# A decoder layer's router: exponential from a hyperbolic tangent, an earlier table load, and the first expert's two products in front of its low parts

## The reference, cut to what matters

```python
logits = x @ router_weight.T + router_bias              # 512 tokens x 16 experts
top_val, top_idx = jax.lax.top_k(logits, 4)
top_val = jax.nn.softmax(top_val, axis=-1)
router_scores = zeros_like(logits).at[arange(T)[:, None], top_idx].set(top_val)
gate_up = einsum('th,ehd->etd', x, gate_up_proj) + gate_up_proj_bias[:, None, :]
gate = minimum(gate_up[..., ::2], 7); up = clip(gate_up[..., 1::2], -7, 7)
glu = gate * sigmoid(gate * 1.702)
out = einsum('etd,edh->eth', (up + 1.0) * glu, down_proj) + down_proj_bias[:, None, :]
out = (out * router_scores.T[:, :, None]).sum(axis=0)
```

## Time and profile before

| what | value |
|---|---|
| median of 3 runs | 230.55 us (229.61 to 231.19) |
| the profiled execution's own time | 230.47 us |
| its span | 228.6 us |
| granted TensorE clock, mean of the span | 0.993 |
| PE busy | 216.3 us (95%) |
| DVE, ACT, POOL busy | 173.0, 127.8, 87.8 us |

### The profile page before, as it was taken

How to read it: one execution, slowest core, us unless ns; L and a number is a source line. 1 busy time by engine, 2 the same in 40 slices (tenths; PEclk the granted TensorE clock), 3 DMA queues, 4 the chain that set the end, 5 groups by cost and what they waited for, 6 DMA issues and landing times.

```text
span 228.6 us, 4527 instructions
## 1 busy us (share of the span) xinstructions
PE 216.3 (95%) x1466; PEld 180.2 (79%) x1466; DVE 173.0 (76%) x434; ACT 127.8 (56%) x247; POOL 87.8 (38%) x67
## 2 busy tenths in 40 slices
PE   7899989998799799989999999999999999999995
PEld 2577857876478599768878988988988988998994
DVE  3489876779357755688798898898889789779655
ACT  2128999874343412835847657566476485395440
POOL 6622269941001100044254455447428428428000
PEclk9999999999799999999999999999999999999999
DMA  5993042000000000004214304404412322310002
GB/s 145 323 409 125 1 140 94 3 4 0 0 0 3 0 0 3 1 0 139 67 73 139 133 4 138 138 7 131 138 40 97 138 57 80 138 46 0 0 3 92
DMA packets 7998, 17.43 MB, mean 76 GB/s; under 512 B 928, under 2 KB 3120, under 8 KB 7856
## 3 DMA queue, kind: packets, MB, share of 16 engines
q1 hardware_dynamic: 7232, 16.52, 21.5%
q10 hardware_dynamic: 752, 0.73, 1.3%
HBM read 16.72 MB, written 0.52 MB: 75 GB/s over the span
## 4 chain that ended last, share of the span: by engine, by line
PE 74%; DVE 10%; ACT 6%; DMA 4%; issue 3%; ACTq 1%; DVEq 0%
PE PS L1121 35%; PE PS L1137 19%; DMA mask<-mask_d 4%; PE PS L1008 3%; PE PS L993 3%; ACT pr L418 3%; DVE masked L692 2%; PE PS L964 2%; PE PS L950 2%; PE PS L981 2%; PE PS L1166 2%; PE PS L1088 1%; DVE HL L813 1%; PE PS L936 1%; PE PS L1020 1%
## 5 line engine op out<-in xcount | busy, mean ns | idle before, releaser
L301 POOL TENSOR_TENSOR WLg<-raw_g,WHg 128x1024 fp32r<-128x1024 f32 x16 | 41.1, 2570 | 61.1 <-ACT WHg L388 61.1
L1121 PE MATMUL PS<-XH,WHg 128*128 128x512 f32 x120 | 47.0, 392 | 0.4 <-ACT pt L503 0.4
L1121 PE MATMUL PS<-XL,WHg 128*128 128x512 f32 x120 | 46.9, 390 | 0.0
L1121 PE MATMUL PS<-XH,WLg 128*128 128x512 f32 x120 | 46.7, 389 | 0.0
L813 DVE TENSOR_TENSOR HL<-pt,HH 128x512 fp32r<-128x512 f32 x30 | 30.8, 1026 | 12.2 <-ACT HH L512 12.2
L512 ACT ACTIVATE HH<-pt 128x512 fp32r<-128x512 f32 x30 | 18.9, 631 | 36.7 <-DVE pt L808 35.7
L808 DVE SCALAR_TENSOR_TENSOR pt<-pt 128x512 f32<-128x512 f32 x30 | 36.2, 1205 | 4.2 <-DVE pt L804 1.6
L1137 PE MATMUL PS<-WHd,HH 128*128 128x256 f32 x120 | 34.2, 285 | 0.9 <-DVE HL L813 0.8
L1137 PE MATMUL PS<-WLd,HH 128*128 128x256 f32 x120 | 34.0, 283 | 0.0
L1137 PE MATMUL PS<-WHd,HL 128*128 128x256 f32 x120 | 33.9, 283 | 0.0
L308 POOL TENSOR_TENSOR WLd<-raw_w,WHd 128x512 fp32r<-128x512 f32 x15 | 22.1, 1473 | 16.7 <-ACT WHd L394 16.7
(11 more groups left out here) (149 smaller groups left out, 357.9 us busy)
## 6 DMA issues: line engine op xcount, KB each, us to landing
raw_g<-we_d SPq DMA_DIRECT2D x16, 512.0 KB, 3.9
raw_w<-we_d SPq DMA_DIRECT2D x16, 256.0 KB, 2.7
ctxT<-ctxT_d SPq DMA_DIRECT2D x1, 1024.0 KB, 11.6
ctx_sb<-ctx_d SPq DMA_DIRECT2D x1, 1024.0 KB, 13.7
wqkv<-wqkv_d SPq DMA_DIRECT2D x3, 256.0 KB, 6.5
out_d<-x SPq DMA_DIRECT2D x4, 128.0 KB, 1.8
rows<-rows_d ACTq DMA_DIRECT2D x1, 264.0 KB, 6.3
x<-x_d ACTq DMA_DIRECT2D x2, 128.0 KB, 3.1
```

What stands on the lines that cost most here:

```text
L301: g.tensor_tensor(WLg[slot][:, :, :, :].rearrange("p k g f -> p (k g f)"), raw_g[slot][:, :], WHg[slot][:, :, :, :].rearrange("p k g f -> ...
L1121: i = t.matmul(PS[:, 2 * m + part, :], w[slot][:, k, part, m * P:(m + 1) * P], xx[:, k, :], start=(n == 0), stop=(n == 3 * KD - 1))
```

## The change

Three things are changed.

1. `elog` becomes tanh(`dlog` / 8). DVE works the exponential out of it: with t = tanh(d / 8), (1 + t) / (1 - t) = exp(d / 4), whose fourth power is exp(d). That takes five more DVE instructions on 128 x 64 values: 1 - t (`root`), its reciprocal, (1 + t) times that, and two squarings.
2. The table set that holds the gate's function and the tangent is loaded by a `preload_act_table_set` in ACT's code, after `context_take(3)`.
3. In expert 0, DVE runs `product(0)`, `product(1)`, `low(0)`, then the copy of `scoreT`, then `low(1)`. Before it ran `product(0)`, the copy, `low(0)`, `product(1)`, `low(1)`. The other experts keep their order.

```diff
@@ scalar engine
             context_take(3)
+            a.preload_act_table_set("gelu_apprx_sigmoid_and_others")
             act.wait_ge(xs_done, NC)
             high_tokens(6, 10, slice(S, S + P), xh_done)
             high_tokens(4, 11, slice(S + P, T), xh_done)
             act.wait_ge(dlog_done, 1)
-            a.activation(elog[:, :, :], dlog[:, :, :], ACT.Exp).then_inc(elog_done, 1)
+            a.activation(elog[:, :, :], dlog[:, :, :], ACT.Tanh, scale=0.125).then_inc(elog_done, 1)
@@ vector engine, router
             link(i)
+            dve.wait_ge(elog_done, 1)
+            v_.tensor_scalar(root[:, :, :], elog[:, :, :], -1.0, 1.0, ALU.mult, ALU.add)
             link(v_.tensor_tensor(within[:, :, :], rank[:, :, :], need[:, :].unsqueeze(2).to_broadcast([P, NC, E]), ALU.is_le))
+            v_.reciprocal(esel[:, :, :], root[:, :, :])
             link(v_.tensor_tensor(sel_eq[:, :, :], eq[:, :, :], within[:, :, :], ALU.mult))
+            v_.scalar_tensor_tensor(out=root[:, :, :], in0=elog[:, :, :], scalar=1.0, in1=esel[:, :, :], op0=ALU.add, op1=ALU.mult)
             link(v_.tensor_tensor(sel[:, :, :], sel_eq[:, :, :], gt[:, :, :], ALU.add))
-            dve.wait_ge(elog_done, 1)
+            link(v_.tensor_tensor(esel[:, :, :], root[:, :, :], root[:, :, :], ALU.mult))
+            link(v_.tensor_tensor(elog[:, :, :], esel[:, :, :], esel[:, :, :], ALU.mult))
             link(v_.tensor_tensor(esel[:, :, :], elog[:, :, :], sel[:, :, :], ALU.mult))
@@ vector engine, expert
                 product(0)
                 if isinstance(e, int) and e == 0:
+                    product(1)
+                    low(0)
                     dve.wait_ge(scoreT_ps, 1)
                     v_.tensor_copy(scoreT[:, :], PS[0:E, 5, :]).then_inc(scoreT_done, 1)
-                low(0)
-                product(1)
-                if isinstance(e, int) and e == 0:
                     low(1)
...
                 else:
+                    low(0)
+                    product(1)
                     weighted_sum(e - 1, 1 - slot, (0, 1))
```

More of the change, by code:

```diff
@@ L130, in decoder_layer @@
         elog = sb("elog", [P, NC, E])
+        root = sb("root", [P, NC, E])
         esel = sb("esel", [P, NC, E])
```

## The result

The changed kernel took 227.51 us (median of 4 executions, 227.01 to 229.01), the kernel before 230.76 in the same comparison; the ratio is 0.9897, with a 95% interval of 0.9856 to 0.9937. I had forecast 229.1 with a range of 228.4 to 230.3. The profiled execution took 227.48 us with a span of 225.5, against 230.47 and 228.6.

A forecast was written before the change was run, and what follows sets the result against it. PE, busy 216.3 of 228.6 us, was taken as the bound; with the earlier gate and expert 0's new order, `down(0)` starts 1.4 us earlier, so 230.47 - 1.4 = 229.1 us, range 228.4 to 230.3.

The forecast's parts named there:

- A: DVE score chain, expert 0: five more instructions for the tangent delay `score` by 1.2 us, ends 0.9 and 1.45.
- E: DVE, expert 0: the first product ends at 96.0 us against 94.95 before, 1.05 us later.
- (b): DVE, expert 0: `low(0)` loses its race with POOL, `down(0)` comes 0.95 us later, 231.4 us; chance 0.04.
- (c): DVE score chain: tangent costs more, delaying `low(1)`; with the reciprocal 0.7 us dearer, 229.9 us; chance 0.12.
- (d): PE before `gate_up(1)`: only the table load's move pays, at most 0.43 us, 230.0 to 230.5 us; chance 0.10.
- (a): Later experts: POOL holds DVE's second product in every one, DVE sets the pace, 231.5 us; chance 0.06.
- the size of the prize: PE's idle time before `gate_up(1)` (0.43 us) and `down(0)` (0.83 us), together 1.26 us, about 0.5% of the time.

The follow-up runs named there:

- tangent-only run: Changed kernel with expert 0's DVE work in its old order, plus eight matmuls on zeros in PE's idle stretches at 56.5 and 58.5 us; 229.85 us.
- order-only run: Kernel before with only expert 0's new DVE order, plus eight matmuls on zeros in PE's idle stretches at 56.5 and 58.5 us; 227.91 us.
- filling the wait: Kernel before with eight matmuls on zeros at 56.5 and 58.5 us, plus two before `gate_up(1)` and four before `down(0)`; median 228.96 us.
- warmed changed kernel: Changed kernel plus eight matmuls on zeros in PE's idle stretches at 56.5 and 58.5 us; 227.12 us, then 227.44 us when timed again.
- warming the first place alone: Kernel before plus eight matmuls on zeros in PE's idle stretches at 56.5 and 58.5 us, no others; 229.66 us, then 230.02 us.
- warmed kernels: All kernels, before, changed or partly changed, given eight more matmuls on zeros in PE's idle stretches at 56.5 and 58.5 us; 227.12 to 230.02 us.

## Why the prediction was wrong, point by point

**The edit's own worth was right.** Forecast was -1.4 us, with 1.1 to 1.6 as its own range; measured was D + 11.57 to D + 10.04, -1.53. Step by step, with the forecast positions counted from D = 90.59:

- The gate no longer holds PE: `gate_up(1)` starts at 91.12 - 89.04 = D + 2.08 (forecast 92.7, which is D + 2.1). The load, at 79.80, is hidden.
- A, the price of the tangent up to `score`, is 4.01 - 2.85 = 1.16 us (forecast 1.2). The reciprocal is 0.55 us long and 0.47 to the next start, against 0.45 taken.
- E, the end of the first product, is 94.40, D + 5.36 (forecast D + 5.4).
- The first low part starts 0.65 us ahead of POOL (forecast 0.6), and the second ends at D + 9.99 (forecast D + 10.06). That 0.07, and rounding in the sum, make the 0.1 us that the edit gave more than forecast.

The rivals did not come about: (b), the first low part took 0.69 us; (c), the reciprocal was as taken; (d), `down(0)` moved by the whole 1.53; (a), POOL's low parts of later experts alternate as before (2.39 us at 128.04, 2.91 at 136.67), and PE shows no wait behind `down(0)`. Without the tangent's arithmetic PE's own work sets the same start (D + 10.02), so both reasons met there, as forecast.

Two smaller slips. "That is the size of the prize" put it at 1.26 us, the idle times of the earlier trace rows. These are counted from the modelled end of a matmul. From start to start the edit took 0.59 us out ahead of `gate_up(1)` (2.67 to 2.08 from D), 0.88 between the biases and `down(0)` (2.82 to 1.94) and 0.06 in between, 1.53 in all. And rival (c) leaves a gain of about 0.75 us by its own figures, not 0.6.

The race between DVE and POOL goes as the Trainium skill has it in "SBUF — State Buffer", section "Who interferes with whom": of two operations that contend, the one that starts first is not disturbed. In the tangent-only run POOL started at 96.31 and the product at 96.45 was held for 2.77 us; in the earlier trace rows DVE started first, at 139.70, and POOL's part was stretched to 2.91. In the order-only run the first `HL`, at 94.77, was over 0.06 us after POOL's start at 95.40, and neither was stretched. That they share ports is what that section says; the runs show only that one stands while the other works.

**The step that failed is the base of the sum**: "230.47 - 1.4 = 229.1 us, on the profiled execution's own time". That execution had a stretch of half clock from 60.0 to 63.4 us, worth 1.55 us, and I took it for a fixed part of the kernel. The granted clock of 0.993 beside the span said so, as did the page's clock row, a 7 among nines in one of 40 slices; I read busy times and waits and passed both over. The stretch is a matter of chance from one execution to the next: 26 of 72 executions of the kernel before have none. From a base at full clock, 228.9, the same -1.4 gives 227.5, the median measured. "A median of a few runs may stand 0.5 us off" was the same mistake in the range: with groups 1.5 to 1.7 us apart, a median of four stands in one group or the other, and the first comparison set three of four executions after at full clock against a median of before that by its time (230.76) belongs to the slower one. How far the first measurement lay from the forecast is in part luck, then: the next twelve executions of the changed kernel have a median of 228.51, inside the range, and all sixteen 228.3, just below it.

**A second effect was missed.** PE's wait before `down(0)` is not only 0.83 us lost. It is also a place where the clock falls, during the wait or up to 0.9 us after it: two traces show it, filling the wait took the executions at full clock from 7 of 21 to 10 of 12, and without the wait they are 18 of 21, all 12 of the warmed changed kernel among them. The means are 230.4 for 72 executions before and 228.3 for 16 after, 2.1 us apart; 1.4 to 1.5 of that are the path, and the other 0.6 fit the rarer half clock (8 of 16 executions below full clock, against 46 of 72), though 16 executions don't fix that number.

**What stays open.** Why the clock falls in one execution and not in the next, with the same busy time in the stretch before (0.70 and 0.69 us of PE in the 2 us ahead of 60 us). Why warming the first place alone brings no more executions at full clock is open too. And the place at 34.2 to 37.6 us, seen once, was not tried.

## What to carry to other kernels

Look at the granted clock of the profiled execution before its time becomes the base of a sum: where it is below 1.00, find the stretch, price it, and ask whether other executions have it. Compare executions of like mean clock, and put instructions at the same distance from a mark just ahead of the edit, so that what happened earlier drops out. Where an operation of DVE can be held by one of POOL, order the DVE work so that what POOL will hold is the last operation before a wait, not one on which others hang; such an order and an earlier release can be worth more together than apart.

## What the runs showed of the hardware

- In a share of the executions TensorE's clock falls to half during a wait of 0.8 to 1.3 us or up to 0.9 us after it, for some 3.4 us, which costs 1.5 us. Of the warmed kernels 22 of 30 executions with such a wait before `down(0)` were below full clock, 3 of 21 without it, 2 of 12 with it filled.
- A reciprocal of 128 x 64 on DVE took 0.55 us, where a product of the same shape took 0.22 (`score`, at 93.05).
- An operation of DVE with two inputs in SBUF that started 0.14 us after POOL's of 2.36 us took 2.77 us in place of 0.69, and ended 0.55 us after POOL's. The copy of `scoreT`, which reads PSUM, took 0.68 us beside POOL.
- A table load of 1.28 us is started ahead of the wait of the activation that it serves, and hides in it (86.09, with the activation at 89.31).
